# One prepared sum for the last layer's chunks, another VectorE order in the final steps, and another bank for one up product

## The reference, cut to what matters

```python
for i in range(DEPTH):                                   # DEPTH = 6
    x = attn_layer(shift_tokens(x), ...) + x
    x = ffn_layer(shift_tokens(x), ...) + x              # a * gelu(gate) @ W2 + b2
return x
...
x = x + _L0_attn_ref(xn, ...) + _L0_ffn_ref(xn, ...)     # input + dense attention + stack
```

## Time and profile before

| what | value |
|---|---|
| median of 3 runs | 2293.3 us (2289.16 to 2295.18) |
| profiled execution, its own time | 2290.97 us |
| its span in the profile | 2289.2 us |
| granted TensorE clock, mean | 0.971 |
| busy: PE, DVE, ACT, POOL | 92%, 87%, 77%, 57% of the span |

### The profile page before, as it was taken

The page is one execution under the profiler, slowest core; times in us unless marked ns, Lnnn a source line. Parts: engine busy times, 40 slices in busy tenths (PEclk is TensorE's granted clock), DMA queues, the critical chain, the costliest instruction groups (busy, mean ns, idle before and its releaser), DMA issues. The chain is left out here.

```text
span 2289.2 us, 69852 instructions
## 1 busy us (share of the span) xinstructions
PE 2109.1 (92%) x28313; PEld 1292.0 (56%) x28313; DVE 1986.0 (87%) x2383; ACT 1773.5 (77%) x4234; POOL 1312.2 (57%) x1084
## 2 busy tenths in 40 slices
PE   5999999999998689999999999899999999999985
PEld 2122222222222577777777777777777777777763
DVE  7999999999990888989898998898898999899973
ACT  3388888888887578878778887888887878788872
POOL 4211101110100777888787887788787888788850
PEclk8699999999999899999999999999999999999998
DMA  2322222222220233353425342433334333433331
GB/s 43 97 65 73 78 71 80 69 82 49 57 73 10 65 81 85 86 134 92 108 72 141 96 101 75 128 93 92 88 89 120 102 90 85 125 92 97 90 87 33
DMA packets 167798, 194.12 MB, mean 85 GB/s; under 512 B 87414, under 2 KB 107508, under 8 KB 167476
## 3 DMA queue, kind: packets, MB, share of 16 engines
q1 hardware_dynamic: 167220, 189.65, 31.8%
q10 hardware_dynamic: 256, 0.00, 0.0%
HBM read 56.98 MB, written 25.42 MB: 36 GB/s over the span
## 5 line engine op out<-in xcount | busy, mean ns | idle before, releaser
L982 DVE TENSOR_REDUCE mx<-S_ps 128x1 f32<-128x1024 f32 x512 | 601.6, 1219 | 24.9 <-PE S_ps L1269 19.4
L730 ACT ACTIVATE PT<-E_ps 128x512 f32<-128x512 f32 x1024 | 533.4, 602 | 101.6 <-PE E_ps L1278 99.1
L646 POOL TENSOR_TENSOR tc<-tc,ts 128x1024 f32<-128x1024 f32 x192 | 463.7, 2415 | 29.1 <-DVE ts L1044 28.6
L654 POOL TENSOR_TENSOR tc<-tc,rs 128x1024 f32<-128x1024 f32 x192 | 362.9, 1912 | 13.8
L1269 PE MATMUL S_ps<-KS,QS 48*128 48x512 bf16 x1024 | 320.8, 400 | 10.0 <-DVE mx L982 4.7
L799 ACT ACTIVATE pr<-B_ps,mxB 128x64 f32<-128x64 f32 x1536 | 325.0, 372 | 3.0 <-DVE mxB L1063 3.0
L1278 PE MATMUL E_ps<-QS,KS 64*128 64x512 bf16 x1024 | 317.1, 383 | 7.4 <-ACT PT L730 5.2
L588 POOL CAST w_cut_b<-w_raw_b 128x512 fp32r<-128x512 f32 (+1 forms) x48 | 27.6, 576 | 511.4 <-DMA w_raw_b<-in_Wqkv 379.4
L1315 PE MATMUL B_ps<-w_qkv,x_cut 128*128 128x512 f32 x576 | 260.6, 452 | 32.8 <-POOL x_cut L601 9.6
L1286 PE MATMUL O_ps<-PT,va 128*32 128x512 f32 x2048 | 273.7, 606 | 0.0
L1278 PEld LDWEIGHTS E_ps<-QS,KS 64*128 64x128 bf16 x1024 | 79.4, 94 | 338.1 <-ACT PT L730 258.8
(11 more groups left out here) (180 smaller groups left out, 3982.1 us busy)
## 6 DMA issues: line engine op xcount, KB each, us to landing
xy<-pc SPq DMA_DIRECT2D x768, 64.0 KB, 2.0
vs<-v SPq DMA_DIRECT2D x96, 384.0 KB, 3.7
Wqkv_cut<-w_cut_b SPq DMA_DIRECT2D x72, 256.0 KB, 2.4
w_qkv<-Wqkv_cut SPq DMA_DIRECT2D x36, 512.0 KB, 7.6
rot<-in_rot SPq DMA_DIRECT2D x96, 128.0 KB, 2.6
vs<-v SPq DMA_DIRECT2D x96, 128.0 KB, 3.8
w_raw_b<-in_Wqkv SPq DMA_DIRECT2D x36, 256.0 KB, 3.0
W_cut<-w_cut_b SPq DMA_DIRECT2D x24, 170.5 KB, 2.4
```

What stands on the lines that cost most here:

```text
L646: e.tensor_tensor(tc[:, :], tc[:, :], m.ts[i][:, :], ALU.add).then_inc(s[f"rot{n}"], 1)
L654: e.tensor_tensor(tc, tc, m.rs[u % 2][2][:, i * H:(i + 1) * H].unsqueeze(2).to_broadcast([P, H, DH]), ALU.mult).then_inc(s[f"{n}_scaled"], 1)
L730: e.activation(m.PT[n % NPT][:, :], turns.bank("probs", n)[:, :], ACT.Exp).then_inc(turns.sem("probs", n), 1)
L982: e.tensor_reduce(m.mx[h % 2][:, i, hf:hf + 1], m.S_ps[n % 2][:, :, :], AX.XY, ALU.max).then_inc(s["sc_max"], 1)
```

## The change

Three things are changed.

1. `final_sum` goes and `final_part` comes. `final_part(c)` adds `stream[1]`, and not `stream[0]`, to `att`, as two instructions of 64 partitions, and it stands at the end of step 4c + 9 (89, 93, 97 and 101), where `final_sum` stood near the start of step 4c + 14 (94, 98, 102 and 106). `residual_2` of the last layer is then one instruction over 128 partitions, `att = (down product + b2) + att`, and it no longer writes `stream[0]`; the transposes wait for it (`down_out`).
2. From step 101 on (`CLOSE`), VectorE's order is: `add_epsilon(23)`, `first_scale(23)`, `ln_root_slope(23)`, `ln_root_fix(23)`, `residual_2(22)`, `final_part(23)`. Before, it was `add_epsilon(23)`, `residual_2(22)`, `first_scale(23)`, `final_sum(22)`, `ln_root_slope(23)`, `ln_root_fix(23)`.
3. The up2 product of chunk 22 alone uses banks 0 and 1 in place of 6 and 7.

```diff
+CLOSE = END + 5
...
+def banks_of(stage, unit):
+
+    return (0, 1) if stage == "up2" and unit == CHUNKS - 2 else BANKS[stage][unit % 2]
...
     def residual_2 (in vector_b)
         bank, cols = banks.one("down", c), m.cols[layer % 2]
         w.wait_ge(s["down_mm"], c + 1)
+        if layer == DEPTH - 1:
+            ac = m.att[:, chunk_cols(g)]
+            w.wait_ge(s["fin_part"], g + 1)
+            e.scalar_tensor_tensor(out=ac, in0=bank, scalar=cols[:, 2:3], in1=ac, op0=ALU.add,
+                                   op1=ALU.add).then_inc(s["down_out"], 1)
+            return
...
-    def final_sum(c):
+    def final_part(c):
...
-        w.wait_ge(s["down_out"], c + 1)
+        w.wait_ge(s["y_out"], 4 * c + 4)
         w.wait_ge(s["att_out"], g + 1)
-        e.tensor_tensor(ac[0:64, :], ac[0:64, :], m.stream[0][0:64, chunk_cols(g)], ALU.add)
-        e.tensor_tensor(ac[64:P, :], ac[64:P, :], m.stream[0][64:P, chunk_cols(g, 1)], ALU.add).then_inc(s["fin_sum"], 1)
+        e.tensor_tensor(ac[0:64, :], ac[0:64, :], m.stream[1][0:64, chunk_cols(g)], ALU.add)
+        e.tensor_tensor(ac[64:P, :], ac[64:P, :], m.stream[1][64:P, chunk_cols(g, 1)], ALU.add).then_inc(s["fin_part"], 1)
...
     for u in range(FIRST, LAST):
         gated(chunk(u - 9), 2)
-        final_sum(late(u - 11))
-        ln_root_slope(chunk(u - 7))
+        if u <= CLOSE:
+            ln_root_slope(chunk(u - 7))
         maxima(tile(u - 3))
...
-        ln_root_fix(chunk(u - 7))
+        if u <= CLOSE:
+            ln_root_fix(chunk(u - 7))
...
         blocks(tile(u - 3))
-        residual_2(chunk(u - 10))
+        if u < CLOSE:
+            residual_2(chunk(u - 10))
         first_scale(chunk(u - 6))
+        if u >= CLOSE:
+            ln_root_slope(chunk(u - 6))
+            ln_root_fix(chunk(u - 6))
+            residual_2(chunk(u - 10))
+        final_part(late(u - 6))
...
     def finish (in tensor_b)
-        w.wait_ge(s["fin_sum"], c % NC + 1)
+        w.wait_ge(s["down_out"], c + 1)
         banks.wait_free(w, "finish", c)
```

More of the change, by code:

```diff
@@ L88 @@
         "mean_mm lnsq var_mm rL_ln rL_exp rL_sq rL_fix rL_x ln_x xl_hi xl_gain xl_lo up_mm0 up_mm1 up_mm2 gelu0 gelu1 gelu2 down_mm "
-        "ld_sums sums_rec st_sums ld_att att_norm att_mm ld_x_c fin_sum fin_T st_out").split()
+        "ld_sums sums_rec st_sums ld_att att_norm att_mm ld_x_c fin_part fin_T st_out").split()
 class Waiter:
@@ L141, in take @@
         if unit is not None:
-            of = BANKS[stage][unit % 2]
+            of = banks_of(stage, unit)
             users[stage, unit] = [last[b] for b in of if b in last]
@@ L318, in one @@
     def one(self, stage, unit):
-        b, = BANKS[stage][unit % 2]
+        b, = banks_of(stage, unit)
         return self.m.ps[b // 2][:, b % 2, :]
     def two(self, stage, unit):
-        return self.m.ps[BANKS[stage][unit % 2][0] // 2][:, :, :]
+        return self.m.ps[banks_of(stage, unit)[0] // 2][:, :, :]
     def wait_free(self, w, stage, unit):
```

## The result

| | median, us | range | runs |
|---|---|---|---|
| before | 2291.72 | 2289.16 to 2295.18 | 5 |
| changed | 2277.89 | 2272.23 to 2286.27 | 5 |

The ratio is 0.9943 (95% interval 0.9917 to 0.9969): 13.8 us faster by the medians, 7 to 19 by the interval. The forecast was 9.0 us faster, 2284.3 with a range from 2280.5 to 2289.0; the time lies 2.6 us under the range. The profiled execution took 2277.00 us, its span 2275.2.

A forecast was written before the change was run, and what follows sets the result against it. After the last projection one chain of waits between engines sets the end; before it PE and DVE are nearly full. +0.3 - 0.8 - 1.8 - 3.15 - 2.2 - 1.4 = -9.0 us off 2293.3 gives 2284.3, range 2280.5 to 2289.0.

The forecast's parts named there:

- Steps 89 to 96: Last layer's projection steps: one more `final_part` costs 1.4 us, `residual_2(20)` saves 0.76; +0.3 taken, bounds +1.4 and -0.8.
- Step 97: Steps 97 and 98, before the last tile's `maxima`: one `residual_2` instruction goes, -0.8 us, at worst 0.
- The bank: `values(95)` starts right after chunk 22's up products, 2.2 us earlier on PE; the table load limits it to -1.8 us.
- (c): Rival, chance 0.03: the instruction behind a table load starts late, `values_out` at 2250.2; +1.4 on the sum, 2285.7 us.
- (e): Rival, chance 0.04: the last tile, not the bank, held PE; leaves out 1.8 us, giving 2286.1.
- Step 101: VectorE's new order from `add_epsilon(23)` on brings `low_ln(23)` earlier: -3.15 us, bounds -4.4 and -2.5.
- The end: From the sum after the last down product to the last transposes, 2.99 us becomes 0.80: -2.2, bounds -2.1 and -2.3.
- The clock in the closing steps: Less idle time raises TensorE's clock: -0.95 us at chunk 23's up product, -0.45 at the last transposes, -1.4 together.
- Rival (a): Chance 0.20: the same chain, but the clock gives nothing back, 0 in place of -1.4; -7.6 us, 2285.7.
- (d): Rival, chance 0.04: PE stays at 1.2 GHz through the closing steps; slower by 11.6 us, 2304.9.
- I take the saving off both: The 9.0 us saving is subtracted from the profiled execution, giving 2282.0, and from the median of 2293.3, giving 2284.3.
- Rival (b): Chance 0.14: projection steps take the full +1.4, half clock on `values(95)` takes 1.6 of the bank's 1.8; -5.0 us, 2288.3.

The follow-up runs named there:

- e6: The changed kernel with `final_part` two steps later (91, 95, 99, 103), behind `low_ln`; ratio 0.9960 to the kernel before, median 2280.15 us.
- e1: The kernel before with only the up2 product of chunk 22 moved to banks 0 and 1; ratio 0.9987, median 2285.33 us.
- e5: The kernel before, unaltered, profiled a second time and timed again; ratio 0.9997, median 2288.99 us.
- e7: The changed kernel with 20 matmuls of a constant, results unread, in PE's idle time; ratio 0.9952 to the kernel before, median 2277.73 us.
- e8: The changed kernel with e6's place of `final_part`, e7's matmuls, and `low_ln(23)` ahead of `final_add(22)`; ratio 0.9940 to the kernel before, median 2275.25 us.

## Why the prediction was right or wrong

**Which regime, which chain: right.** Every piece of the chain that it named moved. Of the closing steps' others, one moved by more than 0.4 us, the variance's 0.70.

**Steps 89 to 96: the number right, in part by luck.** +0.27 against +0.3. The forecast took 0.6, 1.4 less 0.76, and halved it for waits. No wait took anything: the added pair counts whole (1.4), and the saved instruction gives 1.1, more than its own 0.76.

**Step 97: right.** 1.0 us at the last maxima rather than 0.8, and 0.7 or 0.8 where it counts, at the exponentials of the last tile. There ScalarE's `values_out(93)` ends last instead of the maxima. That limit was not named; it is why e6 brought nothing.

**The bank: right,** -1.83 against -1.8, and ScalarE's table load is what is late next. What the forecast didn't have is the 0.70 that the bank gives at the variance behind it, by the clock. On the drain, the row decided rightly: `values_out` starts 0.01 us behind the load in the changed kernel. The drain of about 1380 ns that the Trainium skill gives (ScalarE: Activation LUTs, "What ACT_TABLE_LOAD costs") does not show between a load and the activation behind it here, nor in e1 (load 2252.20 to 2253.48, `values_out` at 2253.49). Rivals (c) and (e) fall.

**Step 101: right, a little small.** -3.57 against -3.15, `low_ln(23)` 6.1 us after the end of `add_epsilon(23)` where 6.5 was forecast. The working let each instruction start after the end of the one before; in the queue of the changed kernel they start 0.6 to 0.7 us after each other, before that end (L1159 at 2255.53, L1178 at 2256.19), and over the five that makes the 0.4. 1.0 of the saving rests on the down product's low clock in the kernel before, as in the row that the forecast used.

**The end: right,** -2.18.

**The clock in the closing steps: right in size by luck,** -1.44 against -1.4. The last transposes gave 0.47, as named (0.45), and so they did in each profile with edit 1. The last up product gave 0.27 and not 0.95: it still ran mostly at 1.2 GHz, and its piece took 12.34 and 12.24 us in the kernel before and 12.07, 11.86 and 12.38 in the changed one. The variance gave the 0.70 that made up for it, by the bank. The reason given, that the shorter idle time ahead of the up product would halve its loss, failed. The other profiles show how loose the sum is: the stretch from the last maxima to `final_add(23)` took 59.07 and 58.80 us in the kernel before, 50.44, 48.63 and 50.47 in the changed one. The pairs differ by 8.3 to 10.4 us, of which the chain's pieces in this stretch make 7.2 (0.39 - 1.83 - 3.57 - 2.18), so 1.1 to 3.2 us are left to the clock. Rival (a), no gain from the clock, is not excluded by time, but the 0.70 and the 0.47 that recur in every changed profile speak against it. (d) did not happen.

**What failed: "I take the saving off both",** the step from the saving to the time, with the bounds set around it. The saving was 9.0, and 16 runs against 83 say 9.3 plus or minus 2.0. But it was taken off 2293.3, the median of three runs, and that kernel's median over 83 is 2288.9; less 9.0 that would have been 2279.9, and the changed kernel's 16 have a mean of 2279.1. By the means, of the 6.4 us between forecast and time 4.9 are the base (2293.3 against 2288.4), 0.3 the saving, and 1.2 the place of the five runs' median, 2277.89, below the mean of 16. The profile's own steps gave a hint that was not priced: 1.2 GHz stretches fall now here, now there, on code that doesn't change, and each is worth 1 to 2 us. In the two first profiles this was 4.6 us (-2.64 and -1.97) in favour of the changed kernel. The range had 3.8 us below the forecast: 2.3 for the bounds of two terms (1.1 and 1.2) and so 1.5 for the spread of the runs, where single runs of one kernel turned out to have a standard deviation of 3.4. Why the five first runs of the kernel before had a median of 2291.7, and those of the three later comparisons 2288.7, 2287.8 and 2289.7, stays open. It can be chance or the chip: the later three ran on three different chips, and the first one's is not known.

**Rival (b)** fell: the addition in the projection steps did count whole, but what was saved counted more than whole, and `values(95)` ran at full clock.

## What to carry to other kernels

In a tail where the engines wait for each other, follow the one chain and count instructions in the queue of the engine that carries it; here the terms for the moved and merged VectorE instructions and for the bank came out within 0.4 us each. When one wait goes, look for what stands a few tenths behind it: a table load capped the bank's 2.2 us at 1.8, and an activation that waits for PE swallowed e6's 1.3 whole. The clock's gain need not come where idle time is removed: the bank's came some 9 us later. Separate the saving from the base: the saving was forecast within the error of 99 runs, the time missed by 6.4 us, and a time can't be better than the median it is subtracted from.

## What the runs showed of the hardware that was not expected

Executions of one kernel, each on one core, differ by 16 us (2278.9 to 2295.2 over 83 runs; 2278.9 to 2294.4 over the 32 of the comparison with e5), and a part of it shows as granted clock on identical instructions: 16.66 us at 1.00 and 18.63 at 0.82. Taking 2.31 us of idle time away ahead of one PE product let another one, some 9 us later and behind the same 1.44 us of idle, run at 2.4 GHz (1.12 us in place of 1.83 to 2.05) in five profiles out of five. Twenty matmuls of a constant in PE's idle time kept it at 1.00 from the last maxima to `final_add(23)` in e7 and e8 (47.12 and 47.57 us); the same and five more in the kernel before did so in part only (0.88 over 57.77 us).
